# One broadcast transfer per block for the reciprocals of a linear-attention kernel, from rows stored side by side

## What is computed

```python
xt = group_norm(x).reshape(16, 256, 6400).transpose(0, 2, 1)
q, k, v = split(xt @ qkv_w.T + qkv_b, 3)
k = k + pos_enc
q, k = relu(q), relu(k)
z  = 1 / (einsum('bic,bc->bi', q, k.sum(axis=1)) + 1e-6)   # per head, per token
kv = einsum('bjc,bjd->bcd', k, v)
out = einsum('bic,bcd,bi->bid', q, kv, z)
y = x + (out @ proj_w.T + proj_b)
```

## Time and profile before

| | |
|---|---|
| runs before, median of 3 | 2761.89 us (2757.27 to 2762.05) |
| the profiled execution's own time | 2772.32 us |
| its span | 2770.5 us |
| TensorE busy | 95% of the span |
| GpSimd, ScalarE, VectorE busy | 70%, 60%, 58% |
| 16 DMA engines, mean busy share | 74.3% (639.18 MB in 357248 packets of the SP queue) |

### The profile page before, as it was taken

One profiled execution on the slowest core, in us unless ns is written; L12 is line 12 of the kernel. 1 busy time (PEld: TensorE's weight loads), 2 busy tenths in 40 slices (PEclk: granted clock), 3 DMA queues, 4 the chain that ended last, 5 costly groups with the idle time before them and its releaser, 6 DMA issues.

```text
span 2770.5 us, 45261 instructions
## 1 busy us (share of the span) xinstructions
PE 2625.4 (95%) x15812; PEld 2230.1 (80%) x15812; DVE 1610.3 (58%) x2525; ACT 1664.1 (60%) x2544; POOL 1929.7 (70%) x1192
## 2 busy tenths in 40 slices
PE   4779999999999999999999999999999999999985
PEld 3667878888887888878888887888888788888864
DVE  5555656656565566656666565565656566655443
ACT  3556656566565656666666665656656566665632
POOL 2436868687676877868687776867768686876842
PEclk9999999999999999999999999999999999999997
DMA  6446878788787887878788787868868787876756
GB/s 223 141 127 196 271 221 259 227 255 252 226 260 222 267 251 225 262 218 263 228 259 262 228 258 225 267 219 259 259 215 263 227 252 234 257 218 202 220 166 183
DMA packets 357471, 642.07 MB, mean 232 GB/s; under 512 B 34432, under 2 KB 55808, under 8 KB 357248
## 3 DMA queue, kind: packets, MB, share of 16 engines
q1 hardware_dynamic: 357248, 639.18, 74.3%
HBM read 519.25 MB, written 119.80 MB: 231 GB/s over the span
## 4 chain that ended last, share of the span: by engine, by line
PE 72%; DVE 10%; ACT 6%; issue 6%; POOL 3%; DMA 2%; SPq 1%; ACTq 0%; DVEq 0%; POOLq 0%
PE psK L514 17%; PE psX L536 15%; PE psX L567 15%; PE psG L526 10%; PE psG L528 5%; PE psT L505 5%; PE psX L553 3%; ACT xn L961 3%; DVE stats L767 2%; DVE psK L784 2%; DVE kk L789 2%; ACT xt L978 1%; POOL hl L1102 1%; POOL q L1120 1%; DVE zt L839 1%
## 5 line engine op out<-in xcount | busy, mean ns | idle before, releaser
L1116 POOL TENSOR_TENSOR kacc<-kacc,kt 128x512 f32<-128x512 f32 x368 | 478.4, 1300 | 380.5 <-ACT kt L990 378.0
L514 PE MATMUL psK<-wqk,hl 128*128 128x256 f32 x4608 | 651.3, 291 | 16.9 <-POOL hl L1102 16.9
L1102 POOL TENSOR_TENSOR hl<-xn,hl 128x512 fp32r<-128x512 f32 x384 | 497.6, 1318 | 243.2 <-ACT hl L973 243.2
L773 DVE TENSOR_TENSOR xt<-psT,xt 128x512 fp32r<-128x512 f32 x400 | 274.7, 687 | 626.9 <-ACT xt L978 626.8
L526 PE MATMUL psG<-kk,xt 128*128 128x512 f32 x1600 | 588.4, 401 | 21.4 <-DVE kk L789 21.4
L536 PE MATMUL psX<-hl,wqk 128*128 128x512 f32 x2304 | 600.4, 396 | 2.2 <-DVE xr L803 2.2
L514 PEld LDWEIGHTS psK<-wqk,hl 128*128 128x128 f32 x4608 | 580.5, 192 | 22.5 <-POOL hl L1102 22.5
L1120 POOL TENSOR_TENSOR q<-q,zb 128x1024 f32<-128x1024 f32 x192 | 461.5, 2404 | 158.3 <-DMA zb<-z_rows 158.3
L567 PE MATMUL psX<-uhl,mhl 128*128 128x512 f32 (+1 forms) x2364 | 557.7, 385 | 11.7 <-DVE uhl L899 11.7
L983 ACT ACTIVATE kk<-psK 128x512 fp32r<-128x512 f32 x400 | 239.8, 600 | 465.3 <-DVE psK L784 459.9
L567 PEld LDWEIGHTS psX<-uhl,mhl 128*128 128x128 f32 x2364 | 435.2, 189 | 103.0 <-DVE uhl L899 12.5
(11 more groups left out here) (112 smaller groups left out, 2354.8 us busy)
## 6 DMA issues: line engine op xcount, KB each, us to landing
zb<-z_rows SPq DMA_DIRECT2D x768, 128.0 KB, 4.4
posb<-pos_plus_bk SPq DMA_DIRECT2D x375, 256.0 KB, 5.4
xs<-in_x SPq DMA_DIRECT2D x184, 512.0 KB, 5.9
xa<-in_x SPq DMA_DIRECT2D x184, 512.0 KB, 6.0
xr<-in_x SPq DMA_DIRECT2D x184, 512.0 KB, 3.9
y<-xr SPq DMA_DIRECT2D x184, 512.0 KB, 6.7
z_rows<-zt SPq DMA_DIRECT2D x32, 256.0 KB, 5.4
posb<-in_pos SPq DMA_DIRECT2D x25, 256.0 KB, 2.8
```

The source lines that it names most:

```text
L514: last = mm(psK[:, par(n, h), i * C:(i + 1) * C], hl_of(t)[:, a, c, s:s + P], wqk[:, w, c, C:2 * C], start=(j == 0), stop=(j == len(terms) ...
L1102: g.tensor_tensor(hl_of(t)[:, 1, :, s], xn_of(n, t)[:, :, s], hl_of(t)[:, 0, :, s], ALU.subtract).then_inc(xl_ready, 1)
L1116: g.tensor_tensor(both, both, kt[:, par(n, h), :], ALU.add).then_inc(ks_done, 1)
```

## The change

The order of the rows in `zt` and `z_rows` is changed: head h of half c now stands on row 32*(t%4) + 8*(t%8//4) + 2*h + c. The two rows of a head are neighbours, and in DRAM they are one run of 1024 numbers. `load_zb` issues one transfer for a block, whose source is 4 heads x 32 copies x 1024 numbers and whose destination is the 128 partitions of the slot. For the tail, two transfers, one for each half, of 4 heads x 32 copies x 256 numbers. Slots alternate over t within a batch, and the tail has a semaphore of its own.

```diff
         def zb_no(n, t):
-            return 16 * HPC * ((NBLK * n + t) // 2 + 1)
+            return 16 * ((NBLK - 1) // 2 * n + t // 2 + 1)
...
             def load_zb(n, t):
 
-                wait(sp, u_ready, blk_no(n, t) - 2)
+                if t > 1:
+                    sp.wait_ge(u_ready, blk_no(n, t - 2))
+                else:
+                    wait(sp, u_ready, blk_no(n - 1, LAST - t))
                 sp.wait_ge(z_stored[t // 8], 16 * (n + 1))
-                k = size(t)
                 r = 32 * (t % 4) + 8 * (t % 8 // 4)
-                rows = zd[t // 8, r:r + 8, 0:k].rearrange("(c h) n -> h c n", c=CC)
-                for h in range(HPC):
-                    sp.dma_start(zb_of(n, t)[32 * h:32 * h + 32], rows[h].partition_broadcast(HD)).then_inc(
-                        zb_landed[(NBLK * n + t) % 2], 16)
+                rows = zd[t // 8, r:r + 8].rearrange("(h c) n -> h c n", c=CC)
+                if t == LAST:
+                    for c in range(CC):
+                        src = rows[:, c, 0:HALF].unsqueeze(1).broadcast_to([HPC, HD, HALF])
+                        sp.dma_start(zb_of(t)[:, c, :], src).then_inc(zb_tail_landed, 16)
+                else:
+                    src = rows.rearrange("h c n -> h (c n)").unsqueeze(1).broadcast_to([HPC, HD, CC * BLK])
+                    sp.dma_start(zb_of(t).rearrange("p c n -> p (c n)"), src).then_inc(zb_landed[t % 2], 16)
...
-                        w = WIN - 8 * s - 4 * c
+                        w = WIN - 8 * s - c
...
-                v.tensor_tensor(swin[:, :, WIN:WIN + HPC], hmask[:].unsqueeze(1).broadcast_to([P, CC, HPC]),
+                v.tensor_tensor(swin[:, :, WIN:WIN + 8].rearrange("p c (h x) -> p c h x", x=2)[:, :, :, 0], hmask[:].unsqueeze(1).broadcast_to([P, CC, HPC]),
                                 bank[:, 0:CC].unsqueeze(2).broadcast_to([P, CC, HPC]),
                                 ALU.mult).then_inc(swin_ready, 1)
...
             def scale(n, t):
-                pool.wait_ge(zb_landed[(NBLK * n + t) % 2], zb_no(n, t))
-                g.tensor_tensor(q_of(n, t), q_of(n, t), zb_of(n, t), ALU.mult).then_inc(u_ready, 1)
+                if t == LAST:
+                    pool.wait_ge(zb_tail_landed, 32 * (n + 1))
+                else:
+                    pool.wait_ge(zb_landed[t % 2], zb_no(n, t))
+                g.tensor_tensor(q_of(n, t), q_of(n, t), zb_of(t), ALU.mult).then_inc(u_ready, 1)
```

More of the change, by code:

```diff
@@ L154, in build @@
         z_stored = [sem(f"z_stored{i}") for i in range(2)]
+        zb_tail_landed = sem("zb_tail_landed")
         zb_landed = [sem(f"zb_landed{i}") for i in range(2)]
@@ L222, in par, with zb_of @@
             return (NHB * n + h) % 2
-        def zb_of(n, t):
-            return zb[:, (NBLK * n + t) % 2, :, 0:size(t)]
+        def zb_of(t):
+            return zb[:, t % 2, :, 0:size(t)]
         def half_no(n, h):
@@ L361, in store_z @@
             def store_z(n, g):
-                if n > 0:
-                    t = 7 if g == 0 else LAST
-                    sp.wait_ge(zb_landed[(NBLK * (n - 1) + t) % 2], zb_no(n - 1, t))
+                if n > 0 and g == 0:
+                    sp.wait_ge(zb_landed[0], zb_no(n - 1, 6))
+                    sp.wait_ge(zb_landed[1], zb_no(n - 1, 7))
+                elif n > 0:
+                    sp.wait_ge(zb_landed[0], zb_no(n - 1, LAST - 2))
+                    sp.wait_ge(zb_landed[1], zb_no(n - 1, LAST - 1))
+                    sp.wait_ge(zb_tail_landed, 32 * n)
                 sp.wait_ge(rc_ready, 4 * n + 2 * g + 2)
```

## The result

The change takes 3527.28 us at the median (3523.31 to 3540.83, 4 runs) against 2761.97 before: ratio 1.278, 95% interval 1.274 to 1.282. Forecast were 3082 us and a range of 2800 to 3450. The time lies above that range. The direction, the four engines and the longer line held; the loss is 765 us where 320 were worked out.

What follows compares the result with a forecast made beforehand. The prediction took TensorE as the bound, with the DMA line taking over beyond a little more than 18 us added per batch. 2772.3 + 296 (15 batches) + 24 (last part) = 3092, or 3082 us on the median; range 2800 to 3450.

Steps and rivals of the forecast that it cites:

- Bound and line: Within a batch: TensorE bounds; SP's transfers queue until y lands, 13.2 us a round; over 18 us more makes DMA the bound.
- Four engines: zb's new transfer: 4 heads outermost at the source, so 4 engines with 131072 bytes each; 2800 to 3450 us, chance 0.80.
- The rate: zb in SP's line: 25 GB/s per engine, 5.2 us a block; the other bound was 15 GB/s, 8.7 us.
- the prediction's sum for a batch: Four engines' line per batch: 12 x 3.06 + 1.5 = 38.2 us more, less 18.5 of cover, leaving 19.7 us.
- the last part: After 2680 us, GpSimd waits for zb: 2.2 us more per block, eleven waits, 24 us.
- cover: Slack within a batch that hides added DMA time: 15.5 us at the seam plus 3, together 18.5 us.
- four engines, and in each other's way: Rival at zb's writes: four engines hinder each other; 18.4 GB/s each gives 3450 us, 15 gives 3777; chance 0.08 above 3450.
- Sixteen engines: Rival for zb's transfer: all 16 engines share it, last part 19 us shorter, 2743 us; chance 0.12, of which 0.09 faster.
- covered: Rival within a batch: four engines, but all 36 us of idle DMA time is cover; 2819 us, no separate chance given.
- Terms put at zero: Whole kernel: the key window, fewer issues and new waits for zb and store_z were each taken to cost nothing.
- the key window: Write of 128 x 8 numbers once per batch, now with gaps: at most 2.3 us in all, put at zero.
- fewer issues: SP's queue: one issue replaces four taking 1.79 us; xs goes out up to 1.3 us sooner, put at zero.

Runs made afterwards that it cites:

- The two runs with stores: Kernel before, with one or three extra 512 KB stores behind the zb of each full block of the first 15 batches: 2842.92 and 3231.24 us.
- 4, 8 and 16 outermost: The change itself (4), and the change with reciprocals stored two or four times in DRAM, giving its source 8 or 16 outermost pieces: 3527.28, 3073.53 and 2802.29 us.
- four issues: The change with its layout, waits and slots kept, but each block's zb spread by four transfers, one per head, of 32 partitions: 2762.1 us, ratio to before 0.9993.
- the rounds: Separate kernels of transfers only, each round waited for: four loads alone 7.9 us, the change's transfer alone 8.0, loads behind it 17.6, behind it written to DRAM 13.1.
- the run with neighbouring partitions: The change with four transfers per block, one per head, each on four engines that by its shapes write 8 neighbouring partitions each: 3360.77 us, ratio 1.2162.

## Why the prediction was wrong in size

*Bound and line: right.* The round of SP that is shown ended when y landed, and with the longer line it took 17.3 us (1379.58 to 1396.91) in place of 13.2. SP's wait for y doubled (57.2 to 113.8 us in the batch), its longest for xn shrank (15.5 to 10.6), and GpSimd and TensorE got the waits that were named, 75.9 and 23.0 us. The two runs with stores, 2842.92 and 3231.24 us, show the same line without zb's shape.

*Four engines: right.* The packets count them exactly, in four kernels: 4, 8 and 16 outermost ran on 4, 8 and 16 engines. The 100 GB/s of four engines alone agree, and one transfer with 16 shares comes within 1.4% of before. That the count has to divide both sides was my assumption; each of these three divides 128, so no run tests it.

*The rate: wrong, and this is the step that failed.* "The bounds for the rate are these two stretches: 25 GB/s gives 5.2 us, 15 GB/s gives 8.7 us. I take 25, because the slow stretch is one with 16 engines on the same two rows and 32 partitions, and the new transfer puts one engine on each row pair." The reason did not hold. Without the repeated rows the change is no faster (3552 us), and with groups of 8 partitions in place of 32 (16 outermost) an engine goes at 16.3 GB/s, as with four issues. Fewer engines did not make each of them faster: in the change an engine brought zb at 16.7 GB/s and a block took 7.8 us where 5.24 were taken; alone it was 23.3 by its packets, 25.1 by the rounds when zb went to DRAM beside loads, and 13.4 by the rounds when it went to SBUF beside them. With 16.7 GB/s the prediction's sum for a batch is 12.5 x 5.67 - 18.5 = 52 us, against 49.7 measured, and with the last part 3572 us against 3527: one term was mis-sized by 2.6 us a block. The rest of the sum held, with a cover that might have come out anywhere from 8 to 23 us. Why an engine goes no faster beside the others stays open beyond what the rounds show, where 4.6 of the 9.8 us that zb adds beside loads go when it is written to DRAM.

*The rival "four engines, and in each other's way"* had the time, at a chance of 0.08 above 3450 us, but hardly the mechanism: alone the four hinder each other little (7.7 us a round against 8.5 and 7.7 for two); the time is lost beside the loads (17.6 us a round against 7.9 for the loads and 8.0 for zb alone). The 167 us between the change and the run with neighbouring partitions, and 7.2 against 9.8 us in the rounds, go the way of a rival in which the place of the writes counts. They don't prove it, since that run also issues later (2.60 us for 0.54), and they leave 279 of the 445 us beyond the forecast to something else. What that is, no run here tells.

*The last part: right,* 23.5 us more where 24 were worked out. There zb has little but stores of y beside it: its packets took 179 ns from 3420 to 3530 us, 22.9 GB/s, near the 25 assumed. *Sixteen engines and "covered":* did not occur. *Terms put at zero:* right for the layout, the key window and the waits together, as the run with four issues shows; what fewer issues alone are worth, no run shows. The run with four issues also shows that 4 KB runs in place of 2 KB gain nothing here: 0.9993.

## What to carry to other kernels

Before joining transfers, count the outermost pieces on *both* sides: a broadcast whose source has 4 outermost ran on 4 of 16 engines. Four transfers of 32 partitions brought the time back (2762.1 us), and copies in DRAM to 16 outermost did so within 1.4%. Price a transfer on few engines by the rate beside the traffic that it will really meet, not by the rate alone: here an engine brought zb at 23.3 GB/s alone, at 16.7 in the kernel and at 13.4 beside loads into SBUF. And where the mean DMA share falls (74.3% to 65.4%) while DMA takes over the chain that ended last (2% to 46%), look whether some engines are idle and others late, as they were here.

## What was not expected of the hardware

The change's transfer, on four engines and written across all 128 partitions, slowed the loads on the other twelve too: all busy at 142 to 233 GB/s together, against up to 407 when it was written to DRAM. And an engine's rate for zb was no higher when 4 in place of 16 shared the transfer: 16.7 against 16.3 GB/s in the kernel.
